# Flamingo gated block on one core: the last set's second norm in two pairs of tiles, its last products in other banks, one store ahead of the last transposes

## What is computed

```python
x = x + tanh(g_xattn) * (ctx @ Wv @ Wout + bout)
h = layernorm(layernorm(x), ln1_g, ln1_b)
h = int8_fake(h) @ ternary_fake(w1).T + b1        # 256 -> 1024; int8 scale from each token's max |h|
h = gelu(h)
h = layernorm(h, ln2_g, ln2_b)                    # the second norm, over 1024
h = int8_fake(h) @ ternary_fake(w2).T + b2        # 1024 -> 256
x = x + tanh(g_ffn) * h
```

## Time and profile before

| | us |
|---|---|
| time, 3 runs: median | 364.4 |
| lowest, highest | 364.04, 367.06 |
| the profiled execution's own time | 364.51 |
| its span, from the first instruction to the last | 362.7 |
| PE, DVE busy in the span | 295.8, 292.4 |
| ACT, POOL busy in the span | 278.7, 265.2 |

### The profile page before, as it was taken

How to read it: one execution, slowest core, us unless ns; L and a number is a source line. 1 busy time by engine, 2 the same in 40 slices (tenths; PEclk the granted TensorE clock), 3 DMA queues, 4 the chain that set the end, 5 groups by cost and what they waited for, 6 DMA issues and landing times. The chain is left out here.

```text
span 362.7 us, 5827 instructions
## 1 busy us (share of the span) xinstructions
PE 295.8 (82%) x1666; PEld 192.4 (53%) x1690; DVE 292.4 (81%) x520; ACT 278.7 (77%) x445; POOL 265.2 (73%) x298
## 2 busy tenths in 40 slices
PE   2987877879899989898999898989898949494565
PEld 1866555345656565556575756565656425242343
DVE  0266873999899989989999999999999958666591
ACT  2154574879898989888989898989898977779340
POOL 4035478879897979787979797979797977748310
PEclk9999988999999999999999999999999978978598
DMA  7955523135958695957666758697373535261468
GB/s 222 316 185 181 159 103 90 58 87 120 171 145 176 148 173 145 176 146 167 154 169 149 174 147 176 146 175 174 74 132 79 127 86 116 68 136 41 77 124 197
DMA packets 98630, 51.56 MB, mean 142 GB/s; under 512 B 87095, under 2 KB 89584, under 8 KB 98598
## 3 DMA queue, kind: packets, MB, share of 16 engines
q1 hardware_dynamic: 97702, 51.14, 59.6%
q10 hardware_dynamic: 896, 0.04, 0.2%
HBM read 21.78 MB, written 8.41 MB: 83 GB/s over the span
## 5 line engine op out<-in xcount | busy, mean ns | idle before, releaser
L392 POOL TENSOR_TENSOR y<-u,g_bc 128x1024 f32<-128x1024 f32 x64 | 151.0, 2366 | 19.7 <-ACT u L569 18.8
L771 DVE TENSOR_TENSOR y<-y,slot_c 128x1024 f32<-128x1024 f32 x64 | 77.6, 1213 | 20.7 <-PE slot_c L1040 20.7
L775 DVE TENSOR_REDUCE amax<-y 128x1 f32<-128x1024 f32 x64 | 77.9, 1218 | 1.8
L550 ACT ACTIVATE q<-y,scale 128x1024 f16<-128x1024 f32 x64 | 69.8, 1142 | 8.0 <-DVE scale L806 8.0
L577 ACT ACTIVATE junk<-u,usum 128x1024 bf16<-128x1024 f32 x64 | 73.5, 1149 | 2.1
L1082 PE MATMUL bank_f<-w2T,q2T 128*128 128x256 f16 x448 | 60.6, 280 | 9.0 <-DVE res L818 5.5
L1082 PEld LDWEIGHTS bank_f<-w2T,q2T 128*128 128x128 f16 x448 | 44.4, 101 | 25.6 <-issue 7.4
L1015 PE MATMUL slot_a<-wvo,ctxT 128*128 128x256 f32 x208 | 54.8, 394 | 0.4 <-ACT ctxT L512 0.3
L1040 PE MATMUL slot_c<-ln_rows,rows 128*128 128x512 bf16 x119 | 37.7, 393 | 17.2 <-DVE y L771 7.7
L569 ACT ACTIVATE u<-slot_a,d 128x1024 f32<-128x1024 f32 x32 | 35.4, 1106 | 10.1 <-PE slot_a L1069 10.0
L1015 PEld LDWEIGHTS slot_a<-wvo,ctxT 128*128 128x128 f32 x208 | 37.4, 196 | 10.7 <-ACT ctxT L512 2.7
(11 more groups left out here) (132 smaller groups left out, 426.7 us busy)
## 6 DMA issues: line engine op xcount, KB each, us to landing
c_in<-in_ctx SPq DMA_DIRECT2D x16, 512.0 KB, 4.5
x_in<-in_x SPq DMA_DIRECT2D x16, 512.0 KB, 3.9
out<-res SPq DMA_DIRECT2D x31, 256.0 KB, 2.7
y<-in_L_ffn_w SPq DMA_DIRECT2D x2, 1024.0 KB, 10.7
u<-in_L_xattn_Wkv SPq DMA_DIRECT2D x2, 512.0 KB, 6.3
u<-in_L_xattn_Wout SPq DMA_DIRECT2D x2, 512.0 KB, 7.9
q2T<-q SPq DMA_TRANSPOSE x64, 3.3
g_bc<-in_L_ffn_ln_g SPq DMA_DIRECT2D x1, 512.0 KB, 5.3
```

What stands on the lines that cost most here:

```text
L392: nc.gpsimd.tensor_tensor(y[:, k % 3, t, :], u[:, t, :], g2_bc[:, :], ALU.mult).then_inc(gain2_done, 1)
L550: nc.scalar.activation(q2[:, t, :], y[:, k % 3, t, :], ACT.Copy, scale=scale[:, (k + 1) % 2, 1, t:t + 1]).then_inc(q2_done, 1)
L771: nc.vector.tensor_tensor(line, line, slot_c[:, :], ALU.add).then_inc(y_done, 1)
L775: nc.vector.tensor_reduce(amax[:, 1, t:t + 1], y[:, k % 3, t, :], AX.X, ALU.max, apply_absolute_value=True).then_inc(amax2_done, 1)
```

## The change

Only the tail is touched; up to body 15 the queues are as before, but for one POOL instruction.

- **Pairs.** The second norm of set 15 (mean, variance, pow, deviation) is done on POOL for tiles 0 and 1 and then for tiles 2 and 3, each with a split, a turn of the rows and a copy of its own: body 16 for the first pair, 17 for the second, and a new body 18 for the inverse scales that set 15's biases need. The first pair's split has only the two numbers of the second norm and two tiles.
- **Gain.** `gain(15, 2)` and `gain(15, 3)` move behind the second pair's split.
- **Queues.** PE, ACT and DVE get a new order for bodies 16 to 18. ACT takes the rows ahead of set 14's quantisation; DVE puts output instructions of sets 13 and 14 between the rows and maxima of set 15; set 14's outputs now wait for all four biases of set 14.
- **Banks.** Set 14's tiles alternate between bank_q and slot_a, and set 15's tile 1 goes to bank_f instead of slot_a.
- **Stores.** On SP, set 13's second store goes ahead of set 14's last transpose, and set 14's first store ahead of set 15's last transpose.

Its core (the waits that only renumber semaphores are left out):

```diff
@@ product_bank
             if k == S - 2:
-                return bank_q[:, half] if t < 2 else slot_a[:, half]
-            return (slot_a[:, 512:512 + D], slot_a[:, 512 + D:1024], slot_b[:, 0:D],
-                    slot_b[:, 512:512 + D])[t]
+                return (bank_q[:, 0:D], slot_a[:, 0:D], bank_q[:, D:2 * D], slot_a[:, D:2 * D])[t]
+            return (slot_a[:, 512:512 + D], bank_f[:, 0:D], slot_b[:, 0:D], slot_b[:, 512:512 + D])[t]
-        bodies = range(-3, S + 2)
+        bodies = range(-3, S + 3)
@@ SP
             turn_second(S - 3, 3)
-            for t in range(T):
-                turn_second(S - 2, t)
-            for t in range(T):
-                turn_second(S - 1, t)
+            turn_second(S - 2, 0)
+            turn_second(S - 2, 1)
+            turn_second(S - 2, 2)
             store(S - 3, 1)
+            turn_second(S - 2, 3)
+            turn_second(S - 1, 0)
+            turn_second(S - 1, 1)
+            turn_second(S - 1, 2)
             store(S - 2, 0)
+            turn_second(S - 1, 3)
             store(S - 2, 1)
@@ POOL
+                def pair_root(h):
+                    two = slice(2 * h, 2 * h + 2)
+                    wait(pool, square_done, T * (S - 1) + 2 * h + 2)
+                    wait(pool, std_done, S + 1 + h)
+                    wait(pool, split_steps, split_count(S - 1 + h))
+                    nc.gpsimd.tensor_scalar(stat[:, 2, two], usum[:, two], -1.0 / H, None, ALU.mult)
+                    nc.gpsimd.tensor_scalar(var[:, 1, two], usq[:, two], 1.0 / float(H) ** 3, LN_EPS,
+                                            ALU.mult, ALU.add).then_inc(var2_done, 1)
+                    wait(pool, var2_done, S + h)
+                    wait(pool, scales_ready, scales_after(S - 2))
+                    nc.gpsimd.tensor_tensor(rstd[:, S % 2, 1, two], var[:, 1, two],
+                                            half_neg[:, 1, two], ALU.pow) \
+                        .then_inc(rstd_done, 1)
...
+                if i == S - 1:
+                    gain(S - 2, 3)
+                    gain(S - 1, 0)
+                    gain(S - 1, 1)
+                    pair_root(0)
+                    return
+                if i == S:
+                    pair_root(1)
+                    return
+                if i == S + 1:
+                    gain(S - 1, 2)
+                    gain(S - 1, 3)
+                    return
@@ DVE, final
-                    if k == S - 1:
-                        wait(dve, ffn_done, T * k + (t + 1 if t > 1 else 2))
+                    if k == S - 2:
+                        wait(dve, ffn_done, T * k + T)
+                    elif k == S - 1:
+                        wait(dve, ffn_done, T * k + t + 1)
```

More of the change, by code:

```diff
@@ L581, in body @@
                 if i == S:
+                    take_rows()
                     quantise(S - 2, 0)
                     quantise(S - 2, 1)
-                    take_rows()
                     quantise(S - 2, 2)
-                    quantise(S - 2, 3)
-                    for t in range(T):
-                        quantise(S - 1, t)
                     return
                 if i == S + 1:
+                    take_rows()
+                    quantise(S - 2, 3)
+                    quantise(S - 1, 0)
+                    quantise(S - 1, 1)
+                    quantise(S - 1, 2)
+                    quantise(S - 1, 3)
+                    return
+                if i == S + 2:
                     take_rows()
@@ L776, in row_max, with scales @@
                                             apply_absolute_value=True).then_inc(amax2_done, 1)
-                def scales(kinds=slice(0, 2), those=slice(0, T)):
+                def scales(kinds=slice(0, 2), those=slice(0, T), turn=0):
                     shape = [P, kinds.stop - kinds.start, those.stop - those.start]
-                    base = 3 * (i + 1 + (those.start > 0))
+                    base = 3 * (i + 1 + turn)
                     one = (slice(None), kinds, those)
@@ L1035, in correction @@
                 def correction(k, t):
-                    wait(pe, rows_copied, k + 3)
+                    late = t // 2 if k == S - 1 else 0
+                    wait(pe, rows_copied, k + 3 + late)
                     wait(pe, y_done, T * k + t)
                     for n in range(2):
-                        terms = nc.tensor.matmul(slot_c[:, 512 * n:512 * (n + 1)], rows[:, (k + 1) % 2, t // 2, :],
+                        terms = nc.tensor.matmul(slot_c[:, 512 * n:512 * (n + 1)],
+                                                 rows[:, (k + 1 + late) % 2, t // 2, :],
                                                  ln2_rows[:, t % 2, 512 * n:512 * (n + 1)],
@@ L1074, in second_product @@
                 def second_product(k, t):
-                    wait(pe, final_done, T * k + 2 * (t // 2) if k < S - 2 else 0)
+                    if k < S - 2:
+                        wait(pe, final_done, T * k + 2 * (t // 2))
+                    elif k == S - 1 and t == 1:
+                        wait(pe, final_done, T * (S - 2))
                     if k > S - 3:
@@ L1085, in second_bias @@
                 def second_bias(k, t):
-                    wait(pe, rows_copied, k + 4)
-                    nc.tensor.matmul(product_bank(k, t), rows[:, k % 2, t // 2, :],
+                    late = int(k > S - 3)
+                    wait(pe, rows_copied, k + 4 + late)
+                    nc.tensor.matmul(product_bank(k, t), rows[:, (k + late) % 2, t // 2, :],
                                      b2_rows[:, D * (t % 2):D * (t % 2 + 1)], start=False,
```

112 lines of the change are left out of this document (70 added, 42 removed).

## The result

The changed kernel takes 363.07 us (median of 9 runs, 361.53 to 363.72), the kernel before, on the same chip, 365.34 (9 runs, 364.04 to 367.06). The ratio is 0.9934, 95% interval 0.9915 to 0.9953: 2.3 us or 0.7% faster, less than the 1% that was set as the bound.

What follows compares the result with a forecast made beforehand. The whole tail was taken to hang on set 15. Last product at 354.8 plus 4.4 to the end gave a span of 359.2 against 362.7, 3.5 less, so 364.51 - 3.5 = 361.0 us; range 359.0 to 363.0.

Steps and rivals of the forecast that it cites:

- The case with the largest chance, within 1%: Whole kernel: time within 1% of the kernel before, neither faster nor slower by more; chance 0.5.
- First pair: POOL's norm of set 15's tiles 0 and 1 starts early: first row on DVE at 334.8, 4.3 us earlier.
- Set 13's outputs between: On DVE between set 15's rows: they wait for set 13's last product at half clock, 0.75 us lost.
- Second pair and moved gains: POOL's norm of tiles 2 and 3, then two gains, 4.7 us: covered, third row at 341.4 to 341.6.
- The new wait: DVE waits for set 14's four biases ahead of set 15's last maximum: 0.7 us lost, last scale at 349.3.
- Last product: PE's last product of set 15 starts at 354.8, half clock being likelier; 4.4 us from there to the end.
- One sign of being wrong: Wrong if the turn of the inverse scales on PE, not the last transpose's landing, held the last product.
- The store's wait: DVE's wait for set 13's store before set 15's first output cost the kernel before 0.45 us; it goes away.
- The delay in the kernel before: Third and fourth transpose of set 15 took 4.2 to 4.6 us instead of 3.2: 1.0 of the before time.
- The rival of the grown wait: Half-clock corrections and a late set 13 store make the last maximum 1.5 later: gain 2, 362.5 us; chance 0.2.

Runs made afterwards that it cites:

- the second chip: The changed kernel run again, unaltered, on another chip against the kernel before: 361.12 us, ratio 0.9882.
- The kernel with the stores last: Changed kernel with both moved stores back behind all transposes of SP's queue: 360.95 us, ratio 0.9892 to the kernel before.
- the fill at the end: Changed kernel with twelve matmuls without use around set 15's last products: 359.40 us, ratio 0.9860 to the kernel before.
- order and fill: Changed kernel with set 14's first output behind last scale, its first store behind last transpose, twelve useless matmuls at end: 359.47 us, 0.9864; repeated 359.53, 0.9844.

## Why the prediction was right, step by step

The median, 363.07, lies 0.07 above the range given (359.0 to 363.0), and the second chip's, 361.12, in its middle. The sum was made against a kernel before of 364.4 us, which took 365.34 on the first chip; the measured ratio applied to 364.4 gives 362.0, inside the range, but outside the forecast's own 360.2 to 361.8. The case with the largest chance, within 1%, came true on the first chip; on the second the ratio is 1.2% below one, with an interval on the other side of the bound for the most part. The forecast of 3.5 us compares with 2.3 and 3.5 in time and 2.6 and 3.2 on the tail. With a start of the tail that scatters by 5.7 us, that the time fell so near is in part luck; the marks of the tail are the better witness.

- **First pair:** right where it counts. First row at 10.23 from zero, predicted 10.3. The pow of two elements cost 0.72, between the bounds, not the 1.67 that I took; it made no difference, as said: POOL was ready at 333.77 and ACT free only at 335.1.
- **Set 13's outputs between:** predicted 0.75 of waiting at half clock, measured 0.97. Half clock came where it was expected, from 337.6 to 341.1.
- **Second pair and moved gains:** covered, as predicted; the third row found its correction waiting.
- **The new wait:** mis-sized. Predicted 0.7, measured 1.40. The transpose of set 14's last tile went out when predicted (17.26 against 17.29 from zero) and landed after 3.9 instead of the 3.2 taken from the earlier trace rows; a transfer of 8 KB of code ran at 19.8. That made set 14's output 0.38 late. The other 0.32 is no loss: DVE was through with tile 3's row that much sooner than predicted, and waited. So the last scale was only 0.3 later than predicted. The kernel with the stores last shows what the early store is to blame for: 0.82 of the wait; 0.58 stay.
- **Last product:** predicted 0.6 too early. I took one stretch of half clock, and there were two on end, so the third product took 1.92 and the last started at half clock too; from its start to the end it took 4.65 instead of 4.4. The two together are the 0.9 missing on the tail. In the second profile there was one stretch, as predicted, and a slow transpose in its stead. One sign of being wrong that the prediction named was that the turn of the inverse scales, not the landing, holds the last product. It came in part, by 0.6 us: what held it was tile 2's product at half clock, which stands behind the turn. The sum itself had reckoned with such a chain (354.8, later than the landing at 353.65), so the sign spoke against the prediction's own sum. The Trainium skill's rule (TensorE: Matmul & The Clock Gate, Part 1), that the fall of the clock is not tied to the kernel's start, fits the two profiles of one kernel that differ in it; but in the second the products ahead came up to 1.4 us later, so they don't show that this is the reason.
- **The store's wait:** predicted to be worth 0.45. It was worth nothing (tail 35.61 with the wait back, 35.57 without): in the new order two of four outputs wait for PE anyway.
- **The delay in the kernel before:** the prediction put 1.0 of the before time down to the late landing of the last transpose. That was misread, though nothing was added up from it. PE goes from tile 1's product at 354.91 to the last at 357.85 without a gap, and DVE hung on the store until 358.41. What counted was that the last transpose took 2.19 to issue, which held the store.
- **The rival of the grown wait** (gain of 2 us) was nearest in time on the first chip, but not by its mechanism: the second pair's corrections ran at full clock (0.59) and set 13's store went out when predicted. The wait grew by the landing, and the rest was the clock at the end.

## What to carry to other kernels

Where a drain at the end of a kernel hangs on one norm over several tiles, do the norm for the tiles that are ready: on the tail of the profiles the gain goes away with the early first pair. A store put ahead of a transpose in the same queue waits for its output and makes the transpose wait too; look whether the wait that it removes ends later than something else that is awaited anyway. Once the tail is short of work for TensorE, its clock becomes a term of the sum, and work that keeps it up must not stand in front of a product that is ready. Then each queue in turn is the next bound: with the fill at the end and the code transfer at the same place (25.9 to 26.0), a last scale that came 1.7 earlier shortened the tail by 0.30, and the moved store by another 0.29. Before two profiles are compared, look where in each of them the code transfers fall: the two profiles of the changed kernel differ by 0.5 us on the tail and those of order and fill by 0.6, with these transfers elsewhere.

## What the runs showed of the hardware

- GpSimd's pow: 1.67 us for 8 elements a partition, 0.72 for 2, so by these two points about 0.16 an element and 0.4 besides, an estimate; the mean, the variance and the deviation beside it take 0.19 to 0.23 at either width.
- Transposes of 128x1024 fp16 by DMA land 3.1 to 3.4 us after their issue; all that took longer, 3.7 to 5.7, had a transfer of code in that time or up to 0.4 us ahead of it, and an issue could take up to 2.41 instead of 1.28. Not every transfer of code delayed one.
- A transfer of 16 KB of code came at 27.6 and 22.2 from zero in two profiles of the changed kernel, and at 20.1 and 25.9 in two of order and fill.
- The part of the program ahead of the tail, the same in all kernels, ended between 320.3 and 326.0 us: a scatter larger than the effect studied.
